# A relational graph layer on one core: the order in which the SBUF tensors are allocated

## What is computed

```python
h = jnp.maximum(_layernorm(x, axis=-1), 0.0)          # x: [128, 128, 128]
# per direction, with rel_ids its relations:
h_ = h @ W.T
g = h_ @ Wg.T
vals = (h_[:, :, None, :] + b) * sigmoid(g[:, :, None, :] + bg)
onehot = (adj[..., None] == rel_ids).astype(h.dtype)
out = einsum('bnmr,bmrd->bnd', onehot, vals)
# fwd and bwd: relations 2..40; loop: relation 1, on adj transposed
return x + relu(out_fwd + out_bwd + out_loop)
```

## Time and profile before

| | |
|---|---|
| median of 3 runs | 104.76 us (104.61 to 105.29) |
| profiled execution | 104.03 us, of which the span (first to last instruction) is 102.2 us |
| granted TensorE clock, mean | 0.992 of 2.4 GHz |
| TensorE, weight loads, VectorE, ScalarE, GpSimd busy | 95.4, 91.3, 90.1, 88.6, 85.8 us |
| chain that ended last | TensorE 71% of the span |
| DMA | 25.45 MB, 249 GB/s on the mean |

### The profile page before, as it was taken

One profiled execution on the slowest core, in us unless ns is written; L12 is line 12 of the kernel. 1 busy time (PEld: TensorE's weight loads), 2 busy tenths in 40 slices (PEclk: granted clock), 3 DMA queues, 4 the chain that ended last, 5 costly groups with the idle time before them and its releaser, 6 DMA issues.

```text
span 102.2 us, 2493 instructions
## 1 busy us (share of the span) xinstructions
PE 95.4 (93%) x802; PEld 91.3 (89%) x802; DVE 90.1 (88%) x196; ACT 88.6 (87%) x144; POOL 85.8 (84%) x162
## 2 busy tenths in 40 slices
PE   5986899998999999999999999999999999999960
PEld 2655789797999999999999999999999999999950
DVE  2289989999999999999999999999999788777761
ACT  5075498899799998999899989998999989898990
POOL 2188999999999999999999999999999999991000
PEclk9999999999999999999999999999999999999996
DMA  1899999999999999999999999999945150606345
GB/s 50 242 319 292 290 290 290 291 293 294 293 312 298 328 328 331 311 329 322 333 282 317 271 324 316 327 292 313 345 134 157 58 151 28 184 6 205 103 140 168
DMA packets 50288, 25.45 MB, mean 249 GB/s; under 512 B 866, under 2 KB 50276, under 8 KB 50276
## 3 DMA queue, kind: packets, MB, share of 16 engines
q1 hardware_dynamic: 50000, 25.17, 88.5%
q10 hardware_dynamic: 276, 0.13, 0.4%
HBM read 16.91 MB, written 8.39 MB: 247 GB/s over the span
## 4 chain that ended last, share of the span: by engine, by line
PE 71%; POOL 4%; ACT 3%; issue 1%; DVE 0%; POOLq 0%
PE psum L786 23%; PE psum L764 12%; PE psum L769 12%; PE psum L765 12%; PE psum L751 11%; POOL rstd L339 3%; ACT junk L442 2%; POOL xn L352 1%; ACT gate L436 0%; PE psum L811 0%; DVE dist_sum L628 0%; DVE flag L630 0%; POOLq L362 0%
## 5 line engine op out<-in xcount | busy, mean ns | idle before, releaser
L352 POOL TENSOR_SCALAR xn<-x_all,mean_neg,rstd 128x128 f32<-128x128 f32 x101 | 44.7, 454 | 0.7 <-POOL rstd L339 0.4
L764 PE MATMUL psum<-w_hi,hT_hi 128*128 128x256 f32 x128 | 33.8, 299 | 1.3 <-DVE w_lo L589 0.9
L786 PE MATMUL psum<-vals,mask 128*128 128x128 f32 x256 | 33.6, 275 | 0.1
L421 ACT ACTIVATE psum<-bias_all 128x1024 f32<-128x1024 f32 x32 | 33.1, 1035 | 0.3 <-DVE vals L557 0.3
L786 PEld LDWEIGHTS psum<-vals,mask 128*128 128x128 f32 x256 | 31.0, 191 | 0.2 <-issue 0.2
L765 PE MATMUL psum<-w_lo,hT_hi 128*128 128x256 f32 x128 | 31.0, 277 | 0.0
L524 DVE BATCH_NORM_STATS2 stats<-x_all 128x6 f32<-128x256 f32 x64 | 23.9, 418 | 3.2 <-DMA x_all<-in_x 3.0
L764 PEld LDWEIGHTS psum<-w_hi,hT_hi 128*128 128x128 f32 x128 | 24.1, 188 | 2.0 <-DVE w_lo L589 1.1
L557 DVE TENSOR_TENSOR vals<-psum,gate 128x512 f32<-128x512 f32 (+1 forms) x33 | 21.9, 663 | 3.9 <-ACT gate L436 3.3
L339 POOL TENSOR_TENSOR rstd<-var_eps,minus_half 128x16 f32<-128x16 f32 (+2 forms) x11 | 24.5, 2225 | 0.1
L765 PEld LDWEIGHTS psum<-w_lo,hT_hi 128*128 128x128 f32 x128 | 24.2, 189 | 0.0
(11 more groups left out here) (36 smaller groups left out, 31.3 us busy)
## 6 DMA issues: line engine op xcount, KB each, us to landing
adj_all<-in_adj SPq DMA_DIRECT2D x16, 512.0 KB, 6.8
x_all<-in_x SPq DMA_DIRECT2D x15, 512.0 KB, 6.8
out<-x_all SPq DMA_DIRECT2D x14, 512.0 KB, 6.2
out<-x_all SPq DMA_DIRECT2D x3, 256.0 KB, 2.3
x_all<-in_x SPq DMA_DIRECT2D x2, 256.0 KB, 3.0
out<-x_all ACTq DMA_DIRECT2D x1, 128.0 KB, 2.5
out<-x_all SPq DMA_DIRECT2D x1, 128.0 KB, 2.6
w_raw<-in_L_gnn_W_loop SPq DMA_DIRECT2D x1, 64.0 KB, 2.5
```

What stands on the lines that cost most here:

```text
L352: last = pool.tensor_scalar(xn[:, g % XN, j * D:j * D + D], x_all[:, g * GC + j * D:g * GC + j * D + D], mean_neg[:, b % BATCH_SLOTS, k:k ...
L421: nc.scalar.activation(prod_ps[s].rearrange("p g a d -> p g (a d)"), bias_all[:, :, :].rearrange("p a d -> p (a d)").unsqueeze(1) .to_broa ...
L764: nc.tensor.matmul(to, hi, w_hi[:, :], start=False, stop=False, skip_group_check=True)
L786: last = nc.tensor.matmul(to[:, j * D:j * D + D], mask[:, g % MASKS, j * N:j * N + N], vals[:, s, j * D:j * D + D], start=True, stop=True)
```

## The change

The calls of sb are put into another order. Before: the small tensors stats, var_eps, rstd, mean_neg and minus_half (the last with 16 floats, 64 bytes a partition), then ident, ones, the weights, bias_all, zeros, bias_row and junk. After: w_hi, w_lo, ident, ones, bias_all, zeros, w_raw, w_gT, bias_row and junk come first, the small tensors after them. Shapes and types stay, and so does the total. The instructions of every engine, their waits and their order are the same.

```diff
--- before.py
+++ after.py
@@ -51,6 +51,7 @@
 
 
         SIDE = max(B * D, 2 * NREL * D + 36 * D)
+
         x_all = sb("x_all", [128, SIDE])
         adj_all = sb("adj_all", [128, SIDE], INT32)
         xn = sb("xn", [128, XN, GC])
@@ -59,21 +60,21 @@
         gate = sb("gate", [128, 2, GC])
         vals = sb("vals", [128, 2, GC])
         mask = sb("mask", [128, MASKS, GROUP * N])
+        w_hi = sb("w_hi", [128, 2 * D], FP32R)
+        w_lo = sb("w_lo", [128, 2 * D], FP32R)
+        ident = sb("ident", [128, 128])
+        ones = sb("ones", [128, 128])
+        bias_all = sb("bias_all", [128, 2, D])
+        zeros = sb("zeros", [128, 4 * D], BF16)
+        w_raw = sb("w_raw", [128, 2, 128])
+        w_gT = sb("w_gT", [128, 128])
+        bias_row = sb("bias_row", [128, 2, D])
+        junk = sb("junk", [128, 4, CC], BF16)
         stats = sb("stats", [128, BATCH_SLOTS, BATCH // 2, 6])
         var_eps = sb("var_eps", [128, BATCH_SLOTS, BATCH])
         rstd = sb("rstd", [128, BATCH_SLOTS, BATCH])
         mean_neg = sb("mean_neg", [128, BATCH_SLOTS, BATCH])
         minus_half = sb("minus_half", [128, BATCH])
-        ident = sb("ident", [128, 128])
-        ones = sb("ones", [128, 128])
-        w_raw = sb("w_raw", [128, 2, 128])
-        w_gT = sb("w_gT", [128, 128])
-        w_hi = sb("w_hi", [128, 2 * D], FP32R)
-        w_lo = sb("w_lo", [128, 2 * D], FP32R)
-        bias_all = sb("bias_all", [128, 2, D])
-        zeros = sb("zeros", [128, 4 * D], BF16)
-        bias_row = sb("bias_row", [128, 2, D])
-        junk = sb("junk", [128, 4, CC], BF16)
         dist = sb("dist", [128, CHUNKS])
         dist_sum = sb("dist_sum", [1, 1])
         flag = sb("flag", [1, 1], INT32)
```

## The result

The kernel after takes 105.86 us (median of 6 runs, 105.39 to 106.52), the one before 104.75 us (104.61 to 105.29): 1.010 of the time, 95% interval 1.007 to 1.013. So it is slower, by about 1.1 us, where no change was forecast, and the median lies above the range (104.0 to 105.5). The profiled execution took 105.74 us with a span of 103.9 us, 1.7 more than the 102.2 of before. The median differs by less, since the profiled execution of before was a quick one, 0.7 us under its median.

What follows compares the result with a forecast made beforehand. The prediction took TensorE and GpSimd to bound the kernel together to about 68 us, GpSimd governing, and TensorE alone from 79 us. Every term was put at 0, sum 0, so 104.7 us (A, chance 0.64), range 104.0 to 105.5.

Steps and rivals of the forecast that it cites:

- The bound and its pace: Main loop: TensorE and GpSimd bound together to about 68 us, GpSimd governing at 2.717 us a group; TensorE alone from 79.
- the one on the products: 384 product matmuls reading w_hi and w_lo: new start addresses save between 0 and 2.2 us of TensorE; taken as 0.
- rival C: Products: the slow pace becomes the rule in all groups, 0.9 us added less 0.1 of waits, 105.6 us; chance 0.10.
- The first reason: Products: w_hi and w_lo start alike in quick and slow groups, so the second pace has another cause; supports 0.
- The second: Products: ident and zeros, also shifted by 64 bytes, show no surcharge; supports 0.
- The third: Products: fetching 128-byte lines would make shifted operands cost 0.123 and 0.136 us, where 0.113 and 0.110 stand; supports 0.
- D: ScalarE's junk and the opening pay for the shifted start: up to 1.9 us of ScalarE, 0.1 on the path, 104.6 us; chance 0.08.
- The rule on lines of 16 bytes: Products: a start 64 bytes on is at a line's start in both kernels, so the saving is 0.
- Rival B: Products pay for the 64 bytes: pitch falls to 0.109, GpSimd catches most of the 2.2 us, 104.3 us; chance 0.18.
- The range: Whole kernel: 104.0 (B's 104.3 less 0.3 for spread) to 105.5 us (the highest run plus a part of C).

Runs made afterwards that it cites:

- the first run: Kernel before with 64 bytes of padding ahead of w_hi and behind w_lo, so only these two begin at a multiple of 128 bytes: 105.77 us, 1.011 of before.
- the second run: Kernel after with the same padding around w_hi and w_lo, so only these two begin 64 bytes past a multiple of 128 again: 105.01 us, 1.0005 of before.

## Why the prediction was wrong, step by step

**The bound and its pace.** Right in its numbers: a quick group at 2.69 us, a slow one at 2.74, GpSimd at 2.717. By TensorE's starts in the timeline the 20 groups take 54.39 us, 2.720 each, which is closer to GpSimd than the 2.73 from the chain. What it left out is VectorE, which the earlier trace rows has at 19.72 of 20 us, just above GpSimd's 19.66; the run without the power shows that it can take GpSimd's place. The table above fits GpSimd's pace. GpSimd's 2.717 leaves the products (2.717 - 0.44 - 0.89) / 12 = 0.1156 us each; the runs with a mean pitch up to 0.1166 take the time of before within 0.3%, and from 0.1183 on all are 0.7% to 2.1% slower. Between them lies the step. The two runs that moved one tensor show the edge: over 20 groups the products take 0.16 us (hT_lo shifted) and 0.36 us (w_lo at 0) more than before, and the stretch grows by 0.06 and 0.25 us.

**The step that failed** is the one on the products: "If none of it is, 0. I take 0". The term was bounded on one side only, by what the even start could save against the fillers' 0.109; that it could cost stood in rival C alone, priced from the slow pace of the same kernel, and no row could bound it. The first reason (two paces at the same addresses, so the pace has another cause) doesn't follow: the pace depends on timing and on the address, and at the wrong distance there is no quick pace at all. The second (ident and zeros show no surcharge) is true and stays true after, but says nothing of the products, as the sentence against it had said: only they read 4 bytes for each column in one pass. The third worked out a line of 128 bytes for one operand alone. The load beside it was left out, and it is the other half. The term, put at 0, was 384 x (0.1193 - 0.1151) = 1.6 us of TensorE, slower. Little of that was hidden in the two profiled executions: over the 20 groups of the middle the products took 1.04 us more (30.36 instead of 29.32, from their starts) and the stretch 0.99 us more. The median rose by 1.1 us only. Part of the gap is the opening, which in the profile of the kernel before was the shortest of all kernels with the power (see D below); where the rest went one profiled execution of each kernel can't show.

**The rule on lines of 16 bytes.** The Trainium skill ("SBUF — State Buffer", Specifications) gives lines of 16 bytes, from which I had concluded that a start 64 bytes on changes nothing. The conclusion doesn't hold for the products: the runs with distances of 48 and 80, a whole line to either side of 64, lie at 0.119 and 0.118 us against 0.115. Whether it holds for one stream alone was not tried.

**Rival C** had the place and the sign, and its price of 105.6 us is near the 105.86 measured. In part that is luck: it counted 0.004 us more in 19 groups, 0.9 us, where the products of the profile took about 1.6 us more. Behind the opening all groups now run at 0.119 to 0.120, a third pace that no whole group of the kernel before has there. Its parenthesis named the wrong reason: that w lies right behind mask is no cause, since the first run is as slow with w far from mask, and the second is quick with w behind mask but for a pad of 64 bytes. It had 1 in 10. Against it I had put that the paces change at fixed addresses, the same conclusion as above.

**Rival B** has the sign wrong: the mean pitch of the products went from 0.115 to 0.119, not to 0.109. What it said of GpSimd catching TensorE's gains was not tested in that direction, as no run made TensorE clearly quicker than before (0.1145 us at best).

**D, ScalarE and the opening.** junk and the seeds gained 1%, 12 and 9 ns, which reached nothing, and their own start is not the reason: in the second run they begin at a multiple of 128 and take 1152 and 1035 ns as before, in the first they are shifted and take 1147 and 1028 ns. Nor does the gain go with the pace of the products alone: with hT at 64 and w at 0, a quick run, it is there too (1139 and 1027 ns). What it goes with stays open. The opening lost 0.26 us, with GpSimd's first 16-wide batch of xn as late as TensorE's transposes of it; the products there were slow already before (0.118). The layout need not be the reason: the transposes that stand at 24.63 in the profile of before stand at 24.81 to 25.57 in the six other runs with a mean pitch up to 0.1166 and at 24.82 to 25.70 in the seven with 0.118 and more, powers in place in all.

**The range** ended at "the highest run plus a part of C". With C an unbounded surcharge on 384 matmuls of the bounding engine it should have held all of C.

## What to carry to other kernels

Where TensorE bounds a kernel and takes in float32r at full rate, the start of the moving operand modulo 128 bytes has to be seen together with the start of the operand that is being loaded: measure the pitch of the matmuls (distance of starts, not their length), and try a pad of 64 bytes before believing in a round address. A trace that shows two paces for the same instructions is a warning that their pitch has a cause not yet understood, not a sign that addresses don't matter. Before work is taken off an engine, look at what its next instruction will then run beside: here 2.7 us less in four groups made the kernel 2% slower. And a price that no row bounds has two sides.

## What the runs showed of the hardware that I had not expected

At 2.4 GHz a 256-column float32r matmul, with a 128x128 float32r load beside it, follows the one before after 0.113 us if the two operands begin 64 bytes apart modulo 128, and after 0.118 to 0.120 us at distances of 0, 32, 48, 80 and 96. Loads and matmuls of float32 with 128 columns don't show it (0.110 and 0.111 us in the kernels before and after and with vals shifted, at distances of 0 and 64). That both streams read the same memory and get into each other's way is the natural reading, and the exchange of the two starts speaks for it; no run here took the loads away, so it is not shown. The Trainium skill ("TensorE: Matmul & The Clock Gate", Part 2: What happens when you issue a matmul) says that moving operand and weight load have independent read ports and that the load takes no bandwidth from the running matmul; for the float32 matmuls and transposes the runs agree. The pitch of the float32r products depends on where the loaded operand begins (0.1185 us with it at 0 and 0.1145 us with it at 64, w at 0 in both), which by that statement it should not. Open stays also what makes the second pace of 0.118 us at a distance of 64. It follows a wait of TensorE, lasts two or three groups in the kernel before, one group with w at 0 and hT at 64, and none of the middle's groups with w 128 bytes on, where the first distances of each group are 7, 3 and 3 ns longer instead.

A VectorE tensor_scalar of 128x128 float32 took 0.33 us inside GpSimd's power of 2.9 us, and 0.99 to 1.07 us where it began before one of GpSimd's copies of 128x512 from int32 to float32 (0.61 us) and ended 0.09 us behind it (kernel before against the one without the power).
